# Row transfers in another order, and another start for the blocks of a four-layer transformer

## The reference, cut to what matters

```python
x_norm = modulate(_ln(x), shift_a, scale_a)
q, k, v = split(x_norm @ W_qkv + b_qkv)                        # self-attention, 256 keys
x = x + gate_a * (softmax(q @ k.T * scale) @ v @ W_proj + b_proj)
q_c = _ln(x) @ W_qc + b_qc                                     # cross-attention, 77 keys
k_c, v_c = split(context @ W_kvc + b_kvc)
x = x + softmax(q_c @ k_c.T * scale) @ v_c @ W_cproj + b_cproj
x_norm2 = modulate(_ln(x), shift_m, scale_m)
x = x + gate_m * (gelu(x_norm2 @ W_mlp1 + b_mlp1) @ W_mlp2 + b_mlp2)
```

## Time and profile before

| | |
|---|---|
| median of 3 runs | 3124.36 us (3105.57 to 3130.01) |
| the profiled execution's own time | 3119.53 us |
| its span in the profile | 3117.5 us |
| mean granted TensorE clock | 0.96 of full speed |
| busy: TensorE matmul, VectorE, ScalarE, GpSimd | 95%, 52%, 49%, 21% |
| chain that ended last, by engine | PE 46%, SPq 15%, issue 7%, DMA 6% |

### The profile page before, as it was taken

How to read it: one execution, slowest core, us unless ns; L and a number is a source line. 1 busy time by engine, 2 the same in 40 slices (tenths; PEclk the granted TensorE clock), 3 DMA queues, 4 the chain that set the end, 5 groups by cost and what they waited for, 6 DMA issues and landing times.

```text
span 3117.5 us, 58368 instructions
## 1 busy us (share of the span) xinstructions
PE 2963.0 (95%) x21972; PEld 2312.7 (74%) x21972; DVE 1621.6 (52%) x3345; ACT 1528.5 (49%) x2677; POOL 652.7 (21%) x733
## 2 busy tenths in 40 slices
PE   5999999966999999999999999999999999999997
PEld 4999999964667777777777767777777776776765
DVE  1444444434656656565655555556555555555541
ACT  2444444413455555555555545555555554555552
POOL 2333333320112212211211121112211111111111
PEclk7999999987899999999999999999999999999998
DMA  4111100004353543435345454353443544435421
GB/s 136 33 44 47 32 24 24 16 25 88 81 124 90 105 94 82 106 71 102 86 95 112 85 106 94 91 122 88 105 98 83 105 91 85 108 75 102 96 56 32
DMA packets 339527, 252.36 MB, mean 81 GB/s; under 512 B 126064, under 2 KB 328672, under 8 KB 339248
## 3 DMA queue, kind: packets, MB, share of 16 engines
q1 hardware_dynamic: 336016, 243.51, 35.5%
q10 hardware_dynamic: 3232, 5.12, 0.5%
HBM read 86.45 MB, written 16.97 MB: 33 GB/s over the span
## 4 chain that ended last, share of the span: by engine, by line
PE 46%; SPq 15%; issue 7%; DMA 6%; POOL 2%; DVE 2%; ACT 1%; POOLq 0%; DVEq 0%; ACTq 0%
PE gbank L2038 9%; SPq L1167 9%; PE gbank L1900 5%; PE obank L1970 5%; PE obank L1900 4%; PE score L1936 4%; DMA qc_cat<-qc_hl 4%; PE obank L1907 3%; PE gbank L1985 3%; PE obank L2016 3%; PE gbank L1907 2%; SPq L1176 2%; PE gbank L1894 2%; PE score L1999 2%; PE score L1950 2%
## 5 line engine op out<-in xcount | busy, mean ns | idle before, releaser
L1481 ACT ACTIVATE p_f<-score 128x1024 f32<-128x1024 f32 (+1 forms) x576 | 562.5, 1020 | 442.2 <-PE score L1950 336.3
L1682 DVE TENSOR_REDUCE m_a<-score 128x4 f32<-128x1024 f32 x384 | 460.0, 1220 | 198.2 <-PE score L1936 197.2
L2038 PE MATMUL gbank<-w,h_c 128*128 128x256 f32 x1536 | 438.1, 417 | 0.9 <-ACT h_c L1498 0.9
L2038 PEld LDWEIGHTS gbank<-w,h_c 128*128 128x128 f32 x1536 | 280.5, 200 | 59.7 <-issue 2.0
L902 PE MATMUL m_ps<-m_comb,m_w 128*128 128x256 f32 x2304 | 300.6, 286 | 0.0
L902 PEld LDWEIGHTS m_ps<-m_comb,m_w 128*128 128x128 f32 x2304 | 284.9, 190 | 3.1 <-issue 1.7
L1692 DVE TENSOR_REDUCE m_b<-gbank 128x4 f32<-128x308 f32 x192 | 92.2, 480 | 338.7 <-PE obank L1985 250.0
L585 ACT ACTIVATE m_hf<-m_ps,tab 128x256 f32<-128x256 f32 x192 | 80.7, 471 | 264.1 <-PE m_ps L902 264.1
L536 POOL TENSOR_TENSOR m_hhl<-m_hf,m_hhl 128x512 fp32r<-128x512 f32 x96 | 125.3, 1305 | 397.3 <-DVE m_hhl L741 397.3
L1970 PE MATMUL obank<-p_f,v_s 128*32 128x256 f32 x3072 | 204.5, 397 | 0.0
L1936 PE MATMUL score<-k_cat,q_cat 48*128 48x256 f32 x1536 | 176.7, 326 | 28.8 <-DMA k_cat<-k_hl 12.1
(11 more groups left out here) (226 smaller groups left out, 5286.4 us busy)
## 6 DMA issues: line engine op xcount, KB each, us to landing
k_cat<-k_hl SPq DMA_DIRECT2D x288, 128.0 KB, 3.2
q_cat<-q_hl SPq DMA_DIRECT2D x288, 128.0 KB, 4.2
qc_cat<-qc_hl SPq DMA_DIRECT2D x288, 128.0 KB, 3.6
x_a<-x_after_L SPq DMA_DIRECT2D x48, 256.0 KB, 2.8
res_a<-x_after_L SPq DMA_DIRECT2D x48, 256.0 KB, 4.8
kc_cat<-kc_hl SPq DMA_DIRECT2D x288, 38.5 KB, 2.0
x_after_L<-y_c SPq DMA_DIRECT2D x32, 256.0 KB, 2.2
bias_a<-rows_L SPq DMA_DIRECT2D x48, 128.0 KB, 4.6
```

What stands on the lines that cost most here:

```text
L1481: e.activation(p_f[i % 4][0:n, :], score[i % 2].ap[0:n, :, :].rearrange("p h n -> p (h n)"), ACT.Exp, scale=SCALE).then_inc(ex.sem, 1)
L1682: e.tensor_reduce(m_a[:, :, i::NPAIR].rearrange("p t h -> p h t"), score[i % 2].ap[:, :, :].rearrange("p h (t k) -> p h t k", t=TT), AX.X, ...
L2038: mm = e.matmul(B_DOWN.ap[:, tt, :], h_c[:, k, tt * P:(tt + 1) * P], weights_of(d)["w2"][:, k, :], start=(k == 0), stop=(k == MC - 1))
```

## The change

In SP's loop `key_rows_high(q)` moves from ahead of the two calls for cross queries to behind them. SP no longer waits ahead of its loop, TensorE neither; the first key rows wait for a new semaphore `s_ones`. The memsets of `k_cat` and `kc_cat` go from VectorE, where they stood ahead of the loop, to the end of GpSimd's iteration 1. VectorE's copy that finishes `sel` goes to the end of its iteration 1, and TensorE waits for it in the first `recips_spread`.

```diff
-        s_one, s_sel = nc.alloc_semaphore("b_const"), nc.alloc_semaphore("b_sel")
+        s_one, s_ones, s_sel = (nc.alloc_semaphore(k) for k in ("b_zeros", "b_ones", "b_sel"))
...
             def key_rows_high(q):
                 if not live(q):
                     return
+                if q == 0:
+                    e.wait_ge(s_ones, 1)
...
-            e.wait_ge(s_one, 2)
             for n in range(N_ITER):
...
                 max_out(m, mT_a, 1, q_cat[m % 2], S["A_ml"], S["A_mrow"])
-                key_rows_high(q)
                 cross_query_rows_high(a)
                 cross_query_rows_low(a)
+                key_rows_high(q)
                 query_rows_high(q)
...
                 cross_residual(a)
+                if n == 1:
+                    for i in range(2):
+                        e.memset(k_cat[i][:, :, :].bitcast(F32), -1.0)
+                    e.memset(kc_cat[:, :, :].bitcast(F32), -1.0).then_inc(s_ones, 1)
...
-            for i in range(2):
-                e.memset(k_cat[i][:, :, :].bitcast(F32), -1.0)
-            e.memset(kc_cat[:, :, :].bitcast(F32), -1.0)
...
-            e.wait_ge(s_sel, 5)
-            e.tensor_copy(sel[:, :, :].rearrange("s c m -> s (c m)"), p_f[0][0:64, 0:2 * P]).then_inc(s_sel, 1)
...
                 queries_low(q)
+                if n == 1:
+                    e.wait_ge(s_sel, 5)
+                    e.tensor_copy(sel[:, :, :].rearrange("s c m -> s (c m)"), p_f[0][0:64, 0:2 * P]).then_inc(s_sel, 1)
...
                 e.wait_ge(*sent.at(u))
+                if u == 0:
+                    e.wait_ge(s_sel, 6)
...
-            e.wait_ge(s_one, 2)
-            e.wait_ge(s_sel, 6)
             for n in range(N_ITER):
```

More of the change, by code:

```diff
@@ L1832, in _ @@
             e.memset(v_s[:, :, :, HD:HD + 1], 1.0)
-            e.memset(vc_s[:, :, HD:HD + 1], 1.0).then_inc(s_one, 1)
-            e.wait_ge(s_sel, 5)
-            e.tensor_copy(sel[:, :, :].rearrange("s c m -> s (c m)"), p_f[0][0:64, 0:2 * P]).then_inc(s_sel, 1)
+            e.memset(vc_s[:, :, HD:HD + 1], 1.0)
             for n in range(N_ITER):
```

## The result

The changed kernel takes 3163.77 us (median of 6 runs, 3150.94 to 3173.14) against 3123.85 us of the kernel before (6 runs, 3105.57 to 3133.14). The ratio is 1.0128, with a 95% interval of 1.0092 to 1.0163. The whole interval lies above 1, so the loss is real, if small. The profiled execution is the fastest of the six, 3150.94 us with a mean clock of 0.96; the other five have 0.949 to 0.953. So its profile shows the mechanism, and somewhat too little of the clock's part.

What follows compares the result with a forecast made beforehand. It took TensorE, busy 95%, as the bound, with two gates opened by one SP stream. From the profiled 3119.53 us, -6 (start) +10 (k_cat later) -29 (old falls) +46 (new falls) = +21 gave 3140 us, own range 3120 to 3158.

Steps and rivals of the forecast that it cites:

- the slower rival: At self_plain (L1936) the one long wait costs the clock nearly always: 3190 us, or 3165 at 25 falls; chance 0.25.
- The wait at cross_plain goes, the one at self_plain grows, SP idles for qc_hl.: SP's row stream: SP waits 0.77 us, qc_cat lands 1.8 us earlier, nearly all 26.7 us at cross_plain go.
- The end of k_cat 0.7 us later, +12, taken as +10.: Self_plain's gate: k_cat's transfers end 0.7 us later on average, net +10 us, bounds -14 and +31.
- the one for six iterations: Self_plain's gate: in six iterations PE came late, so the earlier qc_cat counts in full, 6 x 1.3 us, -8.
- the slack of 0.3 us that I gave 25 other iterations: Self_plain's gate: some 25 iterations have 0.3 us of slack, leaving 0.4 us of the shift each, +10 in all.
- The six falls go, -29.: From cross_plain to self_plain: six falls to the lower clock, 4.8 us each, disappear with the waits, -29 us.
- Half of the iterations have a fall, 23 x 2.0 = +46.: Behind self_plain: 23 of 46 iterations get a clock fall of 2.0 us, +46 us, bounds 0 and +96.
- the clock's two terms: PE's clock: -29 us for old falls behind cross_plain that go, +46 us for new ones behind self_plain.
- Start of the blocks, -6.0.: Ahead of the loop: x loaded 6.9 us earlier, normalisation beside GpSimd's memsets +0.9, together -6.0 us, bounds -7 and -2.
- A wait at L1936 doesn't cost the clock: Faster rival, at self_plain: no clock falls there, -25 us, 3095 us, or 3070 if k_cat's end stays; chance 0.28.
- The long wait costs the clock nearly always: The slower rival, at self_plain: 30 falls of 3.2 us, +96, sum +71, 3190 us; chance 0.25.

Runs made afterwards that it cites:

- the order alone: The kernel before with only the new order of SP's rows, start of the blocks as before: 3162.71 us, ratio 1.0151.
- the filled kernel: The changed kernel with four extra dense matmul calls, results overwritten, ahead of the last cross_plain: 3147 us, ratio 1.0099 to the kernel before.
- split: The kernel before with two of k_cat's four high pieces sent ahead of qc_cat's six and two behind: 3091 us, ratio 0.9908.
- idleness in the old order: The kernel before, rows in old order, with SP made to wait for qc_hl ahead of the key rows: 3258 us, ratio 1.0447.
- recips first, split: The kernel before with r_b's two transfers ahead of the load of x and k_cat's high pieces two and two around qc_cat's: 3065.08 us, ratio 0.9849.

## Why the prediction was right in sign and its sum too low

The forecast was 3140 us, +21 against the profiled execution. It came out at +31 there and +40 in the medians: 3163.77 us is inside the whole range that was left (3085 to 3185), 6 us over the forecast's own (3120 to 3158), and over the bound for "within 1%", which had been given the larger chance, 0.50 against 0.32. It is nearly the slower rival's 3165, but not by that rival's terms (25 falls of 2.8 us): there were 24, of 1.7 us on average in the profiled execution and 2.3 in that of the order alone.

**The wait at cross_plain goes, the one at self_plain grows, SP idles for qc_hl.** All as forecast: 26.7 us to 2.1, SP's first qc_cat transfer 0.1 us behind qc_hl, and 45 waits at self_plain, 65 us in place of the "some 50". qc_cat landed 2.5 us earlier, not 1.8, which changed nothing, since the wait there was gone either way. The 18 transfers of the stream come one every 0.70 us (12.55 us for 18), not 0.64, which is the pace inside one call; the shift doesn't use it.

**"The end of k_cat 0.7 us later, +12, taken as +10."** The shift was right, 0.72 us. The sum of it was the largest error: the waits grew by 30 us (27.8 in the 42 iterations), the upper bound that I had given, 31. The step that failed is the one for six iterations, "PE reached k_cat's gate late, so the earlier qc_cat counts in full, -8". PE was late there because the clock had fallen behind cross_plain. With that fall gone it is not late, and waits for k_cat like all others: +0.7 in place of -1.3, 12 us over six. And the slack of 0.3 us that I gave 25 other iterations all but went, since PE, relieved of the first gate, stands in front of k_cat in every iteration: 25 x 0.3, 7 us. With both corrected the sum is +31, against +30 measured. More simply: before, the one gate or the other was shut in nearly every iteration and both hung on the same stream, so a stream that ends 0.7 us later costs 0.7 us in every iteration.

**"The six falls go, -29."** They went, and were worth 33 (6 x 5.5).

**"Half of the iterations have a fall, 23 x 2.0 = +46."** There were 24. Eighteen cost 1.3 us and six 2.6 us, 40 in all, where I had 46; before had one such fall as well. So the clock's two terms came to +6 in the profiled execution and not +17, and the clock was not the larger term: the waits were, with +30. The price was put at 2.0 us "because dense work follows"; the runs show the length of the fall instead (3.4 or 6.8 us here, 10 to 14 us behind cross_plain), at much the same cost for each us of it. In the profile of the order alone (clock 0.952, like the changed kernel's other five runs) the clock's cost is 56 us, so +22, beside +27 of waits. The forecast of +17 lies between, and the median's further 9 us are probably of this kind; no profile of those runs exists. That the sum came within 10 us of the profiled execution is partly luck: the waits were put 20 us too low, the clock 11 us too high.

**"Start of the blocks, -6.0."** The load of x went out 5.8 us earlier on average, not 6.9, and the first key rows about 2 us earlier, and nothing that a time can show. The term that failed most is the normalisation beside GpSimd: I took 0.9 us from a pair beside smaller work, and it cost 3.75. The memsets' own time was over-estimated (5.8, measured 4.2), but they ended at 689.55, not before 688.

**The rivals.** "A wait at L1936 doesn't cost the clock" fell with the profile: of 29 waits of 1.2 us or more there, 20 were followed by a fall, of 13 shorter ones 4, and in the filled kernel none of 42 iterations had one. The Trainium skill, "TensorE: Matmul & The Clock Gate", section "HAM oscillation — how this bites in real kernels", ties the loss of the clock to idle gaps longer than any of these. The measured waits of 1.2 to 2.3 us decide against it here. The section is right in its main point, that such waits are paid twice: once as idle time, once as slow work behind them. "The long wait costs the clock nearly always" was nearer, though no run has its 96 us behind self_plain; 66 is the most.

What the prediction did not see is that the two halves of the change pull in opposite directions. Moving the queries ahead is a gain (split: -30 us; against idleness in the old order: 3258 to 3163). Having SP wait for qc_hl with ready rows behind it is a loss, and the larger one. I had priced the idleness at +10 and blamed the clock's +17 on the order. A fall behind cross_plain costs 5.5 to 6 us and one behind self_plain 1.3 to 2.6 because it lasts longer there. Why it lasts longer stays open: thin matmuls of 48 rows follow there and dense down calls here, but no run varied that alone.

## What to carry to other kernels

When an in-order queue feeds the bound engine through several gates, price a wait that you put into it by the whole shift times every iteration, and look first for ready work to put into it: two of the four key pieces covered this one in the kernel with the keys split, and two transfers moved into an earlier pause were worth 51 us. If two gates hang on one stream, count them as one: how much the engine waits in all is set by the stream's end, and the order only chooses where it waits. Choose the place behind which dense work stands, or move dense work ahead of the gate; it fills the wait and keeps the clock.

## What the runs showed of the hardware

- Idle waits of PE of 0.9 to 2.3 us were followed by falls of the granted clock to 1.2 GHz in 24 of 42 iterations of the changed kernel, and by none in 11; in the filled kernel, with waits of at most 0.5 us, there was no fall. The shortest wait at a gate with a fall right behind it was 0.59 us (recips first, split). A fall lasted 3.4 or 6.8 us behind self_plain and 10 to 17 us behind cross_plain, and cost 0.39 to 0.45 us for each us of it.
- A shift of SP's stream by 0.5 us was worth 137 us one way and 51 us the other. An iteration became 3.3 us longer (51.64 against 48.34) or 1.0 us shorter (47.31): the clock multiplies the shift.
- VectorE's pair of normalisations (128x256) took 4.48 us beside GpSimd's memsets of 128x2048, where it takes 0.73 us alone, and so in all six profiles with the new start; the memsets took 1.8 us each, as on VectorE.
